# Expert gate and up projections as plain float32 matmuls instead of three products of high and low parts

## The reference

```python
h = _layernorm(x, axis=-1) * (1 + cb) + sb
x = x + gb * _L0_ffn_ref(h, gate_kernel, w0_kernel, w1_kernel, wo_kernel)

def _L0_ffn_ref(x, gate_kernel, w0_kernel, w1_kernel, wo_kernel):
    gate_logits = jnp.einsum('ble,en->bln', x, gate_kernel)
    top_k_weights, top_k_indices = jax.lax.top_k(gate_logits, 2)
    softmax_probs = jax.nn.softmax(top_k_weights, axis=-1)
    weights = jnp.zeros_like(gate_logits).at[b_idx, l_idx, top_k_indices].set(softmax_probs)
    layer_w0 = jnp.einsum('ble,neh->blnh', x, w0_kernel)     # 8 experts, 128 -> 256
    layer_w1 = jnp.einsum('ble,neh->blnh', x, w1_kernel)
    intermediate = jnp.einsum('blnh,nhe->blne', jax.nn.silu(layer_w0) * layer_w1, wo_kernel)
    return jnp.einsum('blne,bln->ble', intermediate, weights)
```

## Time and profile before

| | |
|---|---|
| median of 3 runs | 1150.47 us (1148.97 to 1152.23) |
| the profiled execution | 1151.87 us |
| its span, first to last instruction | 1150.1 us |
| mean granted TensorE clock | 0.898 |
| instructions | 15788 |

### The profile page before, as it was taken

One profiled execution on the slowest core, in us unless ns is written; L12 is line 12 of the kernel. 1 busy time (PEld: TensorE's weight loads), 2 busy tenths in 40 slices (PEclk: granted clock), 3 DMA queues, 4 the chain that ended last, 5 costly groups with the idle time before them and its releaser, 6 DMA issues. The chain is left out here.

```text
span 1150.1 us, 15788 instructions
## 1 busy us (share of the span) xinstructions
PE 950.4 (83%) x5228; PEld 529.0 (46%) x5228; DVE 756.2 (66%) x1426; ACT 669.2 (58%) x1202; POOL 451.0 (39%) x573
## 2 busy tenths in 40 slices
PE   2355778999899999999999999989988997876545
PEld 0222113544365555655564465546544655564432
DVE  5426568766877777788778867786788544664232
ACT  1322556566776576667757766676668575545223
POOL 0442103113471352564176417541642535353530
PEclk8555699999999989999999999999999997999555
DMA  8254103000310040114002401140010001100100
GB/s 223 55 127 101 38 28 68 29 1 2 76 30 31 12 102 1 34 40 102 1 1 73 92 5 30 38 95 1 16 38 4 22 4 27 33 7 0 33 0 9
DMA packets 60335, 46.96 MB, mean 41 GB/s; under 512 B 18800, under 2 KB 56528, under 8 KB 58720
## 3 DMA queue, kind: packets, MB, share of 16 engines
q1 hardware_dynamic: 60256, 45.97, 16.5%
HBM read 30.73 MB, written 14.73 MB: 40 GB/s over the span
## 5 line engine op out<-in xcount | busy, mean ns | idle before, releaser
L1161 DVE TENSOR_REDUCE negmax<-scores_for_max 128x2 f32<-128x1024 f32 x256 | 312.4, 1220 | 77.3 <-PE scores_for_max L741 74.5
L949 ACT ACTIVATE probs<-scores 128x1024 f32<-128x1024 f32 x256 | 262.2, 1024 | 99.2 <-PE scores L760 93.3
L1478 POOL TENSOR_TENSOR acc<-acc,scaled 128x512 f32<-128x512 f32 x56 | 73.3, 1309 | 267.4 <-ACT scaled L1033 267.4
L499 PE MATMUL expert_units<-hb_hi,e_lo 128*128 128x512 f32 x256 | 129.1, 504 | 24.9 <-DVE mu L1244 14.2
L818 PEld LDWEIGHTS shared_ab<-eo,mu 128*128 128x128 f32 x1024 | 129.3, 191 | 35.7 <-issue 25.9
L818 PE MATMUL shared_ab<-eo,mu 128*128 128x128 f32 x1024 | 140.4, 280 | 5.6 <-ACT scaled L1033 3.3
L770 PE MATMUL weighted_values<-probs,vaug 128*32 128x512 f32 x1024 | 142.9, 633 | 0.6 <-ACT probs L949 0.5
L985 ACT ACTIVATE th<-expert_units 128x512 f32<-128x512 f32 x128 | 76.4, 597 | 101.6 <-PE expert_units L501 100.3
L1244 DVE SCALAR_TENSOR_TENSOR mu<-th,expert_units 128x512 f32<-128x512 f32 x128 | 87.6, 685 | 70.8 <-ACT th L985 70.0
L1250 DVE TENSOR_TENSOR mu<-mu,expert_units 128x512 f32<-128x512 f32 x128 | 87.6, 685 | 65.4 <-PE expert_units L501 64.7
L741 PE MATMUL scores_for_max<-ks,qs 48*128 48x512 bf16 x512 | 105.4, 408 | 28.7 <-DVE negmax L1161 27.4
(11 more groups left out here) (212 smaller groups left out, 1585.6 us busy)
## 6 DMA issues: line engine op xcount, KB each, us to landing
parts_d<-parts SPq DMA_DIRECT2D x16, 384.0 KB, 2.5
qs<-parts_d SPq DMA_DIRECT2D x16, 384.0 KB, 5.7
ks<-parts_d SPq DMA_DIRECT2D x16, 384.0 KB, 9.6
w<-in_L_ffn_w SPq DMA_DIRECT2D x16, 256.0 KB, 3.6
parts_d<-parts SPq DMA_DIRECT2D x16, 256.0 KB, 2.9
xp<-in_L_attn_x SPq DMA_DIRECT2D x8, 256.0 KB, 3.0
probs<-in_L_ffn_w_kernel SPq DMA_DIRECT2D x2, 1024.0 KB, 9.0
parts_d<-parts SPq DMA_DIRECT2D x16, 128.0 KB, 2.7
```

The lines of the kernel that those rows point to most:

```text
L499: nc.tensor.matmul(out_ap, w_lo, x_hi, start=True, stop=False)
L949: nc.scalar.activation(probs[:, kt % 2, j, :, :].rearrange("p m s -> p (m s)"), se[:, :], ACT.Exp)\
L1161: V.tensor_reduce(negmax[:, g % 2, :, n], sm[:, :].rearrange("p (m s) -> p m s", m=2), AX, ALU.max, negate=True)\
```

## The change

The experts' projections become one plain float32 matmul each, straight from the loaded weights and hb. The split copies e0_hi, e0_lo, e1_hi, e1_lo, hb_hi and hb_lo and all steps that make them are gone: two ACT copies, one DVE and one POOL difference in the setup, and per batch one ACT and one POOL instruction. The weights are loaded into buffers of their own, and hb has a buffer of its own in place of lying over xbn. The semaphore of POOL's setup is gone. The slots of all other steps are the same. hb is now written after the last w0 and w1, and after the router, of the batch before; xn waits for the transposition of the batch before in place of the router; the router's bank is free with `b_hT`.

```diff
-    ("B", "lo"): dict(pool=(39, 63, 89, 122, 157, 186, 215, 238)),
...
-    ("B", "xT"): ("b_hi", lambda: 1), ("B", "gate"): ("b_lg", lambda: 1),
+    ("B", "xT"): ("b_hT", lambda: 1), ("B", "gate"): ("b_lg", lambda: 1),
...
-        e0_hi, e0_lo = sb("e0_hi", [P, NEX * HID], f32r), sb("e0_lo", [P, NEX * HID], f32r)
-        e1_hi, e1_lo = sb("e1_hi", [P, NEX * HID], f32r), sb("e1_lo", [P, NEX * HID], f32r)
+        e0, e1 = sb("e0", [P, NEX * HID]), sb("e1", [P, NEX * HID])
...
-        hb = xbn[:, :, :].rearrange("p t d -> p (t d)")
-        hb_hi, hb_lo = sb("hb_hi", [P, S], f32r), sb("hb_lo", [P, S], f32r)
+        hb = sb("hb", [P, S])
...
             def w0(b, u):
                 if u == 0:
-                    after(pe, "b_lo", b, 1)
+                    after(pe, "b_hT", b, 1)
                 at = slice(u * P, (u + 1) * P)
                 after(pe, "b_mu", b, u)
-                mm3(w0p[:, :], e0_hi[:, at], e0_lo[:, at], hb_hi[:, :], hb_lo[:, :]).then_inc(sig["b_w0"], 1)
+                nc.tensor.matmul(w0p[:, :], e0[:, at], hb[:, :], start=True, stop=True).then_inc(sig["b_w0"], 1)
...
                 after(pe, "b_u", b, u + 1)
-                mm3(w1p[:, :], e1_hi[:, at], e1_lo[:, at], hb_hi[:, :], hb_lo[:, :]).then_inc(sig["b_w1"], 1)
+                nc.tensor.matmul(w1p[:, :], e1[:, at], hb[:, :], start=True, stop=True).then_inc(sig["b_w1"], 1)
...
                 act.wait_ge(s_c2, 16 * N_LATE)
-                nc.scalar.activation(e0_hi[:, :], raw0, ACT.Copy).then_inc(s_sa, 1)
-                nc.scalar.activation(e1_hi[:, :], raw1, ACT.Copy).then_inc(s_sa, 1)
...
-                ("B", "xn"): normalise("b", x1, xbn, "b_nm", "b_xn", lambda b: ("b_gate", b - 1, 1)),
+                ("B", "xn"): normalise("b", x1, xbn, "b_nm", "b_xn", lambda b: ("b_xT", b - 1, 1)),
...
-                ("B", "hT"): modulate("b_hT", m0[:, :], hb, (bmod[:, 0:1], bmod[:, 1:2]), "b_xT",
-                                      lambda b: ("b_in", b, 32), (hb_hi, "b_hi", lambda b: [("b_w0", b - 1, UNITS), ("b_w1", b - 1, UNITS)])),
+                ("B", "hT"): modulate("b_hT", m0[:, :], hb[:, :], (bmod[:, 0:1], bmod[:, 1:2]), "b_xT",
+                                      lambda b: ("b_in", b, 32), None,
+                                      [("b_gate", 1), ("b_w0", UNITS), ("b_w1", UNITS)]),
...
                 link(V.tensor_tensor(wh_lo[:, :], raw_h, as_f32(wh_hi[:, :]), ALU.subtract))
-                link(V.tensor_tensor(e0_lo[:, :], raw0, as_f32(e0_hi[:, :]), ALU.subtract))
...
                 pool.wait_ge(s_sa, SA_END)
-                G.tensor_tensor(e1_lo[:, :], raw1, as_f32(e1_hi[:, :]), ALU.subtract).then_inc(s_sg, 1)
```

More of the change, by code:

```diff
@@ L310 @@
     "a_rc": GROUPS, "a_o": GROUPS, "a_oT": 1, "a_ot": 1, "a_y": 1, "a_x1": 1,
-    "b_in": 32, "b_mv": 1, "b_eps": 2, "b_rstd": 1, "b_xn": 1, "b_xT": 1, "b_hT": 1, "b_hi": 1, "b_lo": 1,
+    "b_in": 32, "b_mv": 1, "b_eps": 2, "b_rstd": 1, "b_xn": 1, "b_xT": 1, "b_hT": 1,
     "b_gate": 1, "b_lg": 1, "b_top": 1, "b_dif": 1, "b_e2": 1, "b_route": 7, "b_w0": UNITS, "b_w1": UNITS,
@@ L446, in adaln_two_layers @@
         s_sa = ctx.enter_context(nc.semaphore("setup_scalar"))
-        s_sg = ctx.enter_context(nc.semaphore("setup_gpsimd"))
         s_md = ctx.enter_context(nc.semaphore("mod_stored"))
         s_ones = ctx.enter_context(nc.semaphore("ones_rows_loaded"))
-        raw0 = probs[:, 0, :, :, :].rearrange("p g m s -> p (g m s)")
-        raw1 = probs[:, 1, :, :, :].rearrange("p g m s -> p (g m s)")
         raw_qkv = x1
@@ L535, in late_loads @@
                 row = lambda name: a[name].rearrange("(o n) -> o n", o=1)
-                const2(raw0.rearrange("p (e h) -> p e h", e=NEX), a["L0_ffn_w0_kernel"].rearrange("e p h -> p e h"))
-                const2(raw1.rearrange("p (e h) -> p e h", e=NEX), a["L0_ffn_w1_kernel"].rearrange("e p h -> p e h"))
+                const2(e0[:, :].rearrange("p (e h) -> p e h", e=NEX), a["L0_ffn_w0_kernel"].rearrange("e p h -> p e h"))
+                const2(e1[:, :].rearrange("p (e h) -> p e h", e=NEX), a["L0_ffn_w1_kernel"].rearrange("e p h -> p e h"))
                 const2(raw_h, a["L1_attn_W_hidden"])
@@ L572, in ready @@
                 sp.wait_ge(s_sa, SA_END)
-                sp.wait_ge(s_sg, SG_END)
                 sp.wait_ge(s_sx, SX_END)
@@ L695, in ready @@
                 pe.wait_ge(s_sa, SA_END)
-                pe.wait_ge(s_sg, SG_END)
                 pe.wait_ge(s_ones, 32 * PARTS)
@@ L903, in ready @@
                 act.wait_ge(s_sv, SV_END)
-                act.wait_ge(s_sg, SG_END)
                 act.wait_ge(s_sx, SX_END)
@@ L912, in copy_in, with modulate @@
                 return run
-            def modulate(name, src, dst, mod, wait, ready, rounded=None):
+            def modulate(name, src, dst, mod, wait, ready, rounded=None, readers=()):
                 shift, scale = mod
@@ L919, in run @@
                     after(act, *ready(b))
+                    after_all(act, *[(reader, b - 1, k) for reader, k in readers])
                     nc.scalar.activation(dst, src, ACT.Identity, bias=shift, scale=scale).then_inc(sig[name], 1)
@@ L1134, in ready @@
                 dve.wait_ge(s_c2, 16 * N_LATE)
-                dve.wait_ge(s_sg, SG_END)
             def norm_stats(key, src, wait, name):
@@ L1486, in _ @@
                 ("B", "rstd"): deviation("b", "b_mv", "b_eps", "b_rstd", "b_nm"),
-                ("B", "lo"): lower(hb, hb_hi, hb_lo, "b_hi", "b_lo"),
                 ("C", "rstd"): deviation("c", "c_mv", "c_eps", "c_rstd", "c_nm1"),
@@ L1501 @@
 SV_SPLIT = 40
-SV_END = 58
-SA_END = 9
-SG_END = 1
+SV_END = 57
+SA_END = 7
 SX_END = 2
```

## The result

The changed kernel takes 1168.51 us (median of four runs, 1167.91 to 1172.74), the kernel before beside it on the same chip 1151.35. The ratio is 1.015, with a 95% interval of 1.012 to 1.019: 17 us slower, where +24 us on the earlier median of 1150.47 us was forecast (1174.5), in the range of 1161 to 1187. The profiled execution took 1167.91 us, with a span of 1166.1 against 1150.1.

What follows compares the result with a forecast made beforehand. The prediction took PE's hand-ordered queue in the middle (190 to 900 us) as the bound. Products +34, setup -8.2 and modulated activations -2 summed to +24 us on 1150.47, so 1174.5 us, range 1161 to 1187.

Steps and rivals of the forecast that it cites:

- What bounds the kernel: 190 to 900 us: PE's queue sets the pace, busy 667.98 of 710 us, so longer instructions are mostly paid.
- Step 1: Experts' 256 products: plain float32 adds 0.16 us of array and 0.17 us of latency each, 41 to 43.5 us.
- Step 2: Experts' products from 190 to 1055 us: PE's waits swallow some of the price, 80% is paid, +34 us.
- half of 13 us: Middle stretch: of 13 us that 32 waits for maxima and exponentials could swallow, half was taken, 6.7 us.
- Step 3: Setup: without the expert-weight splits the first rotation starts 8.2 us earlier, all of it reaching the end.
- dear end: Setup: DVE's hidden-weights difference still takes 5.02 us, until 39.9, so the rotation starts only 6.0 us earlier.
- Step 4: Modulated activations, each batch: hb_hi and hb_lo go, and PE's wait ahead of the router's matmuls with them, -2 us.
- Step 5: Writes of hT and xn, expert-weight loads: the changed waits and buffers cost nothing.
- A: PE's queue: so tightly packed that nothing is swallowed, +43.5 us paid, total +33 us, 1184 us; chance 0.20.
- B: Start of the kernel: the setup gains nothing, 1182 us, or 1192 us with the full price; chance 0.08.
- C: Middle: row-maxima and exponential loops set the pace, PE's waits shrink, -10 us, 1140 us; chance 0.10 including cases up to no change.
- D: Experts' products: plain float32 isn't dearer, 0.48 us of array against 0.70 per group, 1095 us; chance 0.02.

Runs made afterwards that it cites:

- tenth kernel: Changed kernel with row maxima and exponentials over half the keys, scale 0.25, the unused half of probs filled with ones in the setup: 1136.62 us.
- the ninth: Kernel before with row maxima and exponentials over half the keys and a scale of 0.25: 1110.94 us.
- the third: Kernel before with expert-weight splits moved later, nothing removed: ACT's copies ahead of its first work on batch 1, both differences on DVE ahead of batch 1's last rotation: 1145.73 us.
- the eighth: Kernel before with ACT's copies behind the small preparations, DVE's difference ahead of batch 0's last rotation, POOL's ahead of its first row-maxima work: 1142.04 us.
- the first experiment: Changed kernel with the setup's two ACT copies and the DVE and POOL differences put back, written to unused buffers: 1180.8 us.
- second experiment: Kernel before with only the 256 products made plain float32, on the high parts, all splitting kept: 1183.52 us.
- fourth experiment: Kernel before with one pass in place of three for the experts' projections, low parts still made: 1109.93 us.
- seventh experiment: Kernel before with two more one-pass products per projection group, five in all, their results overwritten: 1256.12 us.

## Why the prediction was right, and where it was off

*What bounds the kernel: right, with a softer edge than I gave it.* PE's queue sets the pace when work is added to it, which costs 76 to 89%. Taking from it brings only 33%.

*Step 1, the products: right.* The records are those of the earlier trace rows, at 0.593 us. In the bare chain a group takes 1.12 us against 0.97, +0.15 where 0.17 was worked out. For groups between an exponential's matmul ahead and one of `down` behind, the distance from the start of the one to the start of the other is 1.298 us against 1.144 at the median of 22 cases, and 1.270 against 1.107 at the shortest: +0.15 to +0.16 us, as forecast. I go on with 0.163 us, 41.7 us for 256 groups.

*Step 2, the share paid: right in size, its explanation not shown.* Forecast were 80% or +34 us; the changed products alone cost +33.3 us in the experts' stretch (80% of 41.7), of which the tail gives 1.7 us back, and the medians say 34 us. I had given 6.7 us to PE's waits for maxima and exponentials. The list of waits shows only 2.5 us of that. The tenth kernel against the ninth says that with both loops short 3 us instead of 8 are swallowed (41.7 - 38.8 and 41.7 - 33.3), so some 5 us would belong to those loops (as little as 2, if the clock's share is taken out), though not under their names: a matmul's record lasts on until its result is written, and such time counts as busy. That last reason is argued, not measured. And it is a difference between single profiles that differ by a few us for other causes; the distance of the medians grows by about 6 us once the tenth kernel's extra setup is taken out, which is within reach of their scatter. That 80% are paid is measured; where the other 8 us go stays open, and that the forecast had just this share owes something to luck, since half of 13 us was a choice.

The prediction paid 7 of 8.8 us for the 52 groups from 900 us on, of which 32 are the last batch. With the products alone changed, its eight experts, from first to last tanh, took 76.6 us instead of 74.4: of some 31 groups times 0.16, 5.0 us, 2.2 were paid. By this pair the last batch's share was put too high, and that of the middle too low: 31.1 us for the seven batches ahead of it, 224 groups or 36.5 us, is 85%. Other single executions spread by as much, though: the changed kernel took 78.0 us for its last batch, and the third and eighth kernels, with the products of before, 72.8.

*The tail* behind the last tanh has no change of its own, and was in no step. It is 1.7 us shorter with plain float32 (93.1 us), and 93.7 and 94.5 us with one pass and five. TensorE had 1.2 GHz for 68 us of it instead of 78.5. I hadn't counted on a clock that differs there.

*Step 3, the setup: right.* Forecast 8.2 us, measured 8.8 at the first exponential; the rotation starts at 38.32 where 38.9 was forecast, DVE's difference takes 0.69 us where 0.7 was taken. The step's dear end is out. That the input of batch 1 would be late next was right as well. The Trainium skill ("SBUF — State Buffer", "Who interferes with whom") has a DVE instruction with both inputs in SBUF and a GpSimd instruction that reads SBUF block each other fully, whichever starts second; the trace agrees on both sides, 0.69 us alone and 5.02 us beside POOL's 4.49 in the first experiment. In the eighth DVE's difference over 2048 columns took 2.98 us instead of 2.29, beside a POOL instruction that had started at 43.60 and took 1.15 us.

What the setup is worth at the end is less sure: 8.8 us by the profile, 12 to 14 us by the medians of the first experiment. Between them lies a stretch whose length no step foresaw. From the first exponential to the first tanh the eight kernels with whole maxima and exponentials took 82.7 to 89.3 us, with the same attention work. The difference goes with the moment at which TensorE is granted 2.4 GHz, as the stretches show, here those of after, behind them those of before:

```profile
110.00:130.00 20.00, 14.51 (x90) 2.97 (x90) 13.06 (x14) 12.35 (x15) 4.03 (x10) 0.85 0.12 41
130.00:150.00 20.00, 13.81 (x95) 3.28 (x93) 13.31 (x14) 12.27 (x14) 1.99 (x5) 1.00 0.12 41
```

```profile
110.00:130.00 20.00, 14.47 (x59) 2.03 (x59) 10.49 (x10) 9.21 (x13) 3.21 (x6) 0.50 0.46 96
130.00:150.00 20.00, 14.76 (x97) 3.45 (x99) 14.21 (x16) 12.69 (x15) 1.99 (x5) 0.90 0.12 41
```

At 110 to 130 us the kernel before still ran at 1.2 GHz, the changed one mostly at 2.4. This explains the 2.6 us of the table's second line in kind. It needs no earlier start: the kernels of the second, fourth and seventh experiment issue the same instructions as the kernel before up to the first product of the experts, and have their first exponential within 1 us of it, but by the profile's record of the granted clock it rose at 124.3, 124.5 and 129.0 us, against 134.2 in the kernel before, and the stretch took 83.0, 83.3 and 85.5 us against 86.2. In the first experiment it rose last of all, at 137.4 us, and the stretch was the longest, 89.3 us. So these 2.6 us can't be credited to the change. Whether an earlier start also helps on average stays open: the five kernels with the first exponential at 108 to 109 us took 83.0 to 89.3 us here, the three with an earlier one 82.7 to 83.6.

*Step 4, hb_hi and hb_lo: mis-sized.* -2 us forecast, -4.1 in the profiles and -2.7 in the medians; so it may be no more than scatter. PE's 2.1 us of waiting for hb_hi are down to 0.4, now for hb itself. If there is a rest, it would be ACT's 0.77 us of a batch that I had costed at nothing, since ACT was off the path; that shorter work on ACT helped in the ninth kernel speaks for it, but no run removed that instruction alone.

*Step 5, new waits: right.* ACT, which now waits for the last w0 and w1 and the router before it writes hb, stood idle ahead of that instruction for 1.5 us in all, twice for the transposition, as before.

The terms add up: -8.8 - 2.6 + 29.2 - 1.7 = +16.1 us, the difference of the spans. Against the forecast of +24, products and tail gave 2.4 us less (31.6 against 34), the split of hb 2.1, the setup 0.6, and 2.6 came from the clock's rise: together 7.7 us, all on the same side.

*The rivals.* A, the full price, is not borne out: the experts' stretch grew by 33.3 of 41.7 us in the second experiment, and the changed kernel stays 16 us under A's 1184. B is out by the first. C had the right direction only for a PE with less to do: at 33% passed on, the fourth experiment comes close to its 23%. Had the change lightened PE, C's way of counting would have been the better one. D is out by the records.

## What to carry to other kernels

In this kernel, where one engine is 94% busy in its middle stretch, three quarters to nine tenths of added work were paid, but only a third of what was taken away came back. Don't count a saving at the rate of a cost, and look for the loops that come next. A change that mixes dearer work on the bound with cheaper preparation should be taken apart: here the gain of the preparation was to be had alone, by the order of the setup, and the version that does so is the fastest of those that leave nothing out. Cut two executions at the same events, not at the same times, when you look for where the time went.

## What the hardware showed that I had not expected

- TensorE's granted clock answers to a change of its load. With one pass, its experts' stretch held 110 us at 1.2 GHz against 37.5 with three, and the mean clock over the span was 0.866 against 0.898; the changed kernel's is 0.912. Lighter work on this engine was partly paid back by slower work.
- It rises after the start-up at moments that differ between executions: at 124.3 to 134.2 us in four that had issued the same instructions until then (the kernel before and those of the second, fourth and seventh experiment), and some 3 us of the time go with it.
- An instruction of DVE over 2048 columns took 2.29 us alone, and one over 512 columns 5.02 us beside POOL's.
